# A GRU with its logits: two operands of the state update moved to PSUM, and gathers without their waits on single pieces of TensorE's work

## The reference

```python
x = emb_table[input_ids]                       # 2048 x 50 x 128
xp = einsum('bth,hk->btk', x, kernel) + b_i    # 384 columns: z, r, h
def step(h, xt):
    rec = h @ rec_kernel + b_r
    z = sigmoid(xz + rz);  r = sigmoid(xr + rr)
    hh = tanh(xh + r * rh)
    return z * h + (1.0 - z) * hh
last = state at the last position of the mask
logits = last @ emb_table.T                    # 2048 x 12501, float32
```

## Time and profile before

| | |
|---|---|
| Median of 3 runs | 1263.59 us (1258.02, 1263.59, 1264.37) |
| The profiled execution's own time | 1257.24 us |
| Its span in the profile | 1255.4 us |
| Mean granted clock of PE | 0.983 of full speed |
| Busy: PE, DVE, ACT, POOL | 86%, 64%, 56%, 65% |
| DMA queues: gathers (software), SP's (hardware) | 43.3%, 30.5% of 16 engines' span |

### The profile page before, as it was taken

One profiled execution on the slowest core, in us unless ns is written; L12 is line 12 of the kernel. 1 busy time (PEld: TensorE's weight loads), 2 busy tenths in 40 slices (PEclk: granted clock), 3 DMA queues, 4 the chain that ended last, 5 costly groups with the idle time before them and its releaser, 6 DMA issues.

```text
span 1255.4 us, 17436 instructions
## 1 busy us (share of the span) xinstructions
PE 1078.9 (86%) x6040; PEld 809.2 (64%) x6040; DVE 808.3 (64%) x1491; ACT 697.7 (56%) x1203; POOL 811.1 (65%) x812
## 2 busy tenths in 40 slices
PE   7956778777777777788889999999999999999997
PEld 6853444444444444444478888888887888988876
DVE  6634555555555555555578777778777777777654
ACT  3533334343434343344357777777777778888644
POOL 0007777777777777777777777777777776666100
PEclk9988999999999999999999999999999999999999
DMA  8975555555555555555578888888888889999799
GB/s 283 355 228 159 165 157 166 156 166 158 166 155 167 158 168 156 164 157 168 151 206 286 283 274 286 278 276 289 283 278 284 281 287 306 307 303 306 267 363 332
DMA packets 127494, 294.28 MB, mean 234 GB/s; under 512 B 18096, under 2 KB 33456, under 8 KB 127408
## 3 DMA queue, kind: packets, MB, share of 16 engines
q0 software_dynamic: 51200, 157.34, 43.3%
q1 hardware_dynamic: 76208, 135.84, 30.5%
HBM read 171.30 MB, written 121.81 MB: 233 GB/s over the span
## 4 chain that ended last, share of the span: by engine, by line
POOL 42%; PE 31%; issue 13%; DMA 10%; DVE 3%; ACT 1%; SPq 0%; DVEq 0%; POOLq 0%; ACTq 0%
POOL gathered L351 42%; DMA gathered<-gate_table,index 4%; PE x_ps L496 4%; PE x_ps L497 4%; PE x_ps L498 4%; DMA out_dram<-logits 3%; DMA gate_table<-gates 3%; PE r_ps L416 2%; PE r_ps L428 2%; PE z_ps L428 2%; PE c_ps L416 1%; PE z_ps L416 1%; PE c_ps L432 1%; PE c_ps L428 1%; PE c_ps L429 1%
## 5 line engine op out<-in xcount | busy, mean ns | idle before, releaser
L351 POOL DMA_INDIRECT gathered<-gate_table,index x800 | 809.2, 1011 | 357.5 <-issue 214.4
L601 ACT ACTIVATE gates<-r_ps,zr_bias 128x512 f32<-128x512 f32 (+1 forms) x250 | 151.1, 605 | 244.0 <-PE r_ps L423 191.5
L805 DVE SCALAR_TENSOR_TENSOR c_ps<-c_ps,bias_sb,gates 128x512 f32<-128x512 f32 (+1 forms) x250 | 162.3, 649 | 172.9 <-PE c_ps L423 128.3
L603 ACT ACTIVATE gates<-z_ps,zr_bias 128x512 f32<-128x512 f32 (+1 forms) x250 | 150.8, 603 | 188.3 <-PE z_ps L423 145.5
L416 PE MATMUL r_ps<-ident,gathered 128*128 128x128 f32 x800 | 111.5, 252 | 154.0 <-DMA gathered<-gate_table,index 153.5
L810 DVE TENSOR_TENSOR kept<-gates,state 128x512 f32<-128x512 f32 (+1 forms) x250 | 145.8, 583 | 118.1 <-ACT gates L603 118.1
L625 ACT ACTIVATE logits<-x_ps,nan_row 128x512 f32<-128x512 f32 (+1 forms) x300 | 197.3, 678 | 21.8 <-PE x_ps L498 20.9
L416 PEld LDWEIGHTS r_ps<-ident,gathered 128*128 128x128 f32 x800 | 84.5, 141 | 178.7 <-DMA gathered<-gate_table,index 153.2
L814 DVE SCALAR_TENSOR_TENSOR gates<-gates 128x512 f32<-128x512 f32 (+1 forms) x250 | 146.3, 585 | 57.8 <-ACT gates L607 56.7
L817 DVE TENSOR_TENSOR state<-kept,gates 128x512 f32<-128x512 f32 (+1 forms) x250 | 147.7, 591 | 26.4 <-DVE gates L814 0.5
L607 ACT ACTIVATE gates<-c_ps,bias_sb 128x512 f32<-128x512 f32 (+1 forms) x250 | 149.5, 598 | 16.2 <-PE c_ps L416 15.5
(11 more groups left out here) (100 smaller groups left out, 1570.9 us busy)
## 6 DMA issues: line engine op xcount, KB each, us to landing
out_dram<-logits SPq DMA_DIRECT2D x192, 512.0 KB, 4.3
gate_table<-gates SPq DMA_DIRECT2D x24, 768.0 KB, 4.2
gathered<-gate_table,index POOLq DMA_INDIRECT x800
emb_rows<-in_L_rec_emb_table_dram SPq DMA_DIRECT2D x48, 256.0 KB, 4.7
out_dram<-logits SPq DMA_DIRECT2D x8, 213.0 KB, 3.2
logits<-in_r_input_ids_dram SPq DMA_DIRECT2D x1, 400.0 KB, 6.0
logits<-in_r_input_mask_dram SPq DMA_DIRECT2D x1, 400.0 KB, 6.2
gate_table<-gates SPq DMA_DIRECT2D x2, 192.0 KB, 9.2
```

The costliest lines, as they stand in the source:

```text
L351: nc.gpsimd.indirect_dma_start(gathered[:, q, n, :].bitcast(F32), None, table, bass.IndirectOffsetOnAxis(ap=index[:, g, n:n + 1], axis=0)) ...
L601: nc.scalar.activation(r_sb[:, b, 0:width], r_ps[:, b, 0:width], ACT.Sigmoid, bias=zr_bias[:, 1:2]).then_inc(s_r, 1)
L603: nc.scalar.activation(z_sb[:, b, 0:width], z_ps[:, b, 0:width], ACT.Sigmoid, bias=zr_bias[:, 0:1]).then_inc(s_z, 1)
L805: nc.vector.scalar_tensor_tensor(out=c_bank, in0=c_bank, scalar=bias_sb[:, 1, 2:3], in1=r, op0=ALU.add, op1=ALU.mult).then_inc(s_scaled, 1)
```

## The change

Four edits, in three of the lists.
- z's sigmoid is written in place, into `z_ps`, and both uses of z on DVE (lines 810 and 814) read it there.
- new = (z - 1) * cand goes into the block's bank of `c_ps`, whose sum the tanh has read by then, and the last subtraction (line 817) takes it from there. The candidate itself stays in SBUF.
- The second, third and fourth gather of a block carry no wait. The constant `AHEAD` goes.
- The first gather's wait is written with other terms; (k - 1) * QS + q + 1 is the same number as g - QS + 1.

No instruction other than waits is added or removed, and no order changes.

```diff
-    AHEAD = QS - 1
...
-        z_sb, r_sb, cand = gates[:, 0], gates[:, 1], gates[:, 2]
+        r_sb, cand = gates[:, 1], gates[:, 2]
...
                 g = k * QS + q
-                ahead = g - AHEAD
                 if k > 0:
-                    pool.wait_ge(s_turned, g - QS + 1)
+                    pool.wait_ge(s_turned, (k - 1) * QS + q + 1)
                 for n in range(tiles_of(blk)):
-                    if ahead >= 0:
-                        if n == 1:
-                            pool.wait_ge(s_rec, 2 * ahead + 1)
-                        elif n == 2:
-                            pool.wait_ge(s_rec, 2 * ahead + 2)
-                        elif n == 3:
-                            pool.wait_ge(s_z_in, ahead + 1)
                     nc.gpsimd.indirect_dma_start(
...
                 act.wait_ge(s_z_in, g + 1)
-                nc.scalar.activation(z_sb[:, b, 0:width], z_ps[:, b, 0:width], ACT.Sigmoid, bias=zr_bias[:, 0:1]).then_inc(s_z, 1)
+                nc.scalar.activation(z_ps[:, b, 0:width], z_ps[:, b, 0:width], ACT.Sigmoid, bias=zr_bias[:, 0:1]).then_inc(s_z, 1)
...
-                z, r, new, kept_b, c_bank = (t[:, b, 0:width] for t in (z_sb, r_sb, cand, kept, c_ps))
+                z, r, new, kept_b, c_bank = (t[:, b, 0:width] for t in (z_ps, r_sb, cand, kept, c_ps))
...
-                nc.vector.scalar_tensor_tensor(out=new, in0=z, scalar=-1.0, in1=new, op0=ALU.add, op1=ALU.mult).then_inc(s_new, 1)
+                nc.vector.scalar_tensor_tensor(out=c_bank, in0=z, scalar=-1.0, in1=new, op0=ALU.add, op1=ALU.mult).then_inc(s_new, 1)
...
-                nc.vector.tensor_tensor(h, kept_b, new, ALU.subtract).then_inc(s_state, 1)
+                nc.vector.tensor_tensor(h, kept_b, c_bank, ALU.subtract).then_inc(s_state, 1)
```

## The result

| | before | after |
|---|---|---|
| Median | 1260.8 us (4 runs, 1255.42 to 1264.37) | 1216.91 us (4 runs, 1215.06 to 1218.09) |
| Ratio | | 0.9654, 95% interval 0.9612 to 0.9696 |
| Profiled execution: time, span | 1257.24, 1255.4 us | 1215.06, 1213.0 us |
| First stage, from PE's first block to its 101st | 529.1 us | 499.9 us |
| Second stage, to the 201st | 398.0 us | 383.6 us |

The forecast was 1217 us, with 1207 to 1237 around it. Of the 42.4 us by which the span fell, 29.2 come from the first stage and 14.4 from the second; the third and the start give 0.9, and the tail takes 2.1 back.

What follows compares the result with a forecast made beforehand. POOL's gathers were taken to bound the first two stages (to 1020 us), PE the third. 1257.24 - 28.4 (first stage) - 15 (second) = 1213.8 us, with 3.6 carried over 1217 us; range 1207 to 1237.

Steps and rivals of the forecast that it cites:

- POOL bounds both stages: First two stages, to 1020 us: POOL issues gathers without a pause, 528.8 of 529 us and 397.8 of 398.
- What stretches a gather: POOL beside DVE: two-SBUF-input instructions hold gathers at two points, early and 0.22 us before the end; single-SBUF-input ones don't.
- What line 817 says of an inference: Skill's inference that a tensor_tensor doesn't stall descriptor generation would mean no gain; 0.81 us after line 817 speaks against it.
- First stage, -28.4 us: First stage: all gather stretch goes, 400 x (1.017 - 0.946) = 28.4 us, POOL stays the bound; bounds 0 to 30.
- Second stage, -15 us, PE as the next bound: Second stage: of 22.5 us stretch, 15 gained, stage 383 us, the bound passing to PE; bounds 0 to 18.
- Third stage and after, 0: Third stage and after: PE has no idle time and unchanged work, so 0; shorter gathers only lengthen POOL's wait.
- Dearer operands, 0 with up to 65 ns for line 814: DVE's PSUM operands: 0 for lines 810 and 817, up to 65 ns for 814, hidden; 0, bounds -2 to +3.
- The waits, 0: Removed gather waits: cost nothing while POOL is behind PE, buffer gives nearly the same depth after; 0, bounds -1 to +3.
- Carrying 3.6 us over: Total: four earlier runs' mean lies 3.6 us above the profiled execution; added to 1213.8 us for 1217.
- The rival in which 817 alone keeps its hold: Line 817 still holds gathers, a third of both gains (14 us) goes, 1231 us; chance 0.04.
- The slower rival: Unpaced gathers delay output stores, deciding from about 11 us of landing; at 13 us, 74 us lost, 1291; chance 0.04.

Runs made afterwards that it cites:

- operands_more: Kernel before with z and new moved to PSUM, every gather wait kept, PE's marks on time: 1217.73 us against 1263.18, ratio 0.9637.
- second_paced: Changed kernel with the second, third and fourth gathers' waits put back for second and third stage alone, marks on time: 1218.07 us against 1263.18, ratio 0.9646.
- z_more: Kernel before with z alone in PSUM, new in SBUF, waits kept, marks on time: 1223.20 us against 1261.10, ratio 0.9687.
- operands_only: Kernel before with z and new moved to PSUM, every gather wait kept, PE's marks late: 1381.84 us against 1375.59, ratio 1.0038.
- after_again: The changed kernel itself once more, PE's marks late: 1426.76 us against 1381.12 for the kernel before, ratio 1.0325.

## Why the prediction was right

- **POOL bounds both stages.** Right. The first stage fell to 400 x 1.251 us when the gathers did, and PE still waited 119 us for them in it.
- **What stretches a gather.** Right for the instructions that were changed, and shown from both sides: taken away it goes, put back it returns, and it follows the inputs, not the output. Wrong in two things that didn't touch the sum. There is one point and not two: the 0.22 us behind line 814 were 0.82 behind line 810, and the gather at 409.62, given as one that line 805 left alone, had begun 0.15 us before that line, so at the one point nothing ran beside it; line 822 is the row that bears the reading. And a single SBUF input does hold a gather where the instruction is the state's copy (line 790), which caused 2.7 of the 2.9 us left in the second stage. The sum is safe since it took all stretch from the means (28.4 and 22.5 us) and not by points.
- **What line 817 says of an inference.** The Trainium skill (SBUF — State Buffer, "Who interferes with whom") infers that a `tensor_tensor` does not stall descriptor generation on POOL. The prediction took line 817's hold as speaking against it. The hold is real (the gather at 215.43 lost 0.37 us), but it comes 0.13 us into the gather, and later in it instructions with two SBUF inputs cost nothing; the gather also reads its indices from SBUF, and no run here shows which of its parts was held, so the inference is neither borne out nor refuted. That section's other rule in the Trainium skill, that a DVE instruction with two SBUF inputs contends with a GpSimd instruction that reads SBUF, agrees with every row here that has two.
- **First stage, -28.4 us.** 29.2 measured between PE's blocks.
- **Second stage, -15 us, PE as the next bound.** 14.4 measured; PE's pace of 7.60 us for a pair was the one forecast. My estimate of 0.02 us of remaining stretch for a gather was too high (2.9 us over 300, 0.010), but that changes nothing when PE is the bound.
- **Third stage and after, 0.** The third stage lost 0.5 us; what follows it took 2.1 more (82.2 against 80.1), which wasn't forecast and wasn't looked into.
- **Dearer operands, 0 with up to 65 ns for line 814.** 693 ns against 687 for new, 688 against 692 for h: 6 ns, not 65. The bound from line 805 was much too wide; that line also takes a scalar from SBUF, but whether this is what costs it 757 ns wasn't tried. ACT's z became 25 ns shorter (662 against 687).
- **The waits, 0.** Right by `operands_more` and `second_paced` while PE's marks are on time. Wrong where they are late, a case that the prediction didn't have.
- **Carrying 3.6 us over** from the profiled execution to the median: 1.9 measured (1216.91 - 1215.06). That the forecast of 1217 came out to 0.1 us is luck: the profiled execution was 1.3 us above the 1213.8 of the sum, and the carry 1.7 us below the 3.6.
- **The rival in which 817 alone keeps its hold**, priced at 1231: `z_more` is this case, and took 1223 in the median and 1233.6 in the profiled execution. In the first stage 11.8 of the 28.7 us stayed, not a third.
- **The slower rival** (stores landing late): the median landing went from 4.3 to 5.0 us, far below the 11 at which it would decide.

## What to carry to other kernels

When an engine issues without a pause and its instructions come in two lengths, look what runs beside the long ones, and measure from the other instruction's end to theirs: a constant distance (here 0.82 us) names a suspect. It isn't yet the cause: an instruction that always follows the culprit at once has a constant distance too (here 0.22 us). Count the cases in which the suspect ran at the same place and nothing happened. Price such a release stage by stage against the next bound, since edits don't add once that bound is reached. A wait that costs nothing while its engine is behind can still be worth keeping: with the waits the kernel measured the same in one condition and 3% better in the other.

## What the runs showed of the hardware

**PE's marks can come late.** In the first eight runs the five kernels that were also measured without this took 9% to 17% longer, all 43 executions of the kernel before beside them included (1369 to 1384 us), and in the last four they didn't; one chip was met under both conditions. The records say this much. In the profile of `operands_only`, PE's product for r was issued at 396.36 and its end is modelled at 397.45; ACT, free since 400.2, began r's sigmoid at 403.09, when the mark came (timeline, PE and ACT):

```profile
396.36 1.09 PE L423 MATMUL r_ps<-state,w_rec_sb 128*128 128x512 f32 x2
403.09 0.69 ACT L601 ACTIVATE gates<-r_ps,zr_bias 128x512 f32<-128x512 f32 x1 [2.87 <-remote]
```

The chain of the same profile, by engine: what released a waiting engine is often not found among the records, where the kernel before had none of it.

```profile
PE 48%; another core or an unknown queue 13%; issue 12%; ACT 12%; DVE 10%; DMA 5%; POOL 0%; DVEq 0%; SPq 0%; ACTq 0%; POOLq 0%
```

The trace records some 1030 marks of PE behind the table, and 414 of them come over 0.3 us behind the end of the matmul that sets them; in the profile of the kernel before it is none of 1420, and DVE's and ACT's marks are on time in both. By stage the late ones are 196 of 328, 190 of 412 and 28 of 178, and none of 108 in the logits behind. That fewer marks are recorded (DVE's and ACT's too) shows that these traces are less complete, and matmuls' ends are modelled, so whether the mark is late or the matmul can't be told from them. PE's granted clock was lower as well: 0.90 in the first stage and 0.985 in the second, where the same kernel with marks on time (`operands_more`) had 0.99 and 1.00. But the second stage took 459.2 us against 385.2, which a clock 1.5% lower doesn't explain. What delays the marks, and why the gathers' waits are worth 3% then (the kernel as changed at 1.0325, with waits at 1.0038), is not settled. In the second stage of `after_again` POOL waited 138.6 us for PE's c parts of four blocks back, in 53 waits of up to 4.2 us, and in `operands_only` 69.2 us in 46 of up to 1.8; that goes with gathers let out in bunches, but what is cause and what is effect wasn't tried.

**The gap between gathers is fixed.** 0.30 us, with a wait that is already over or with none, in all kernels. With 946 ns for a gather of 128 rows, POOL took 1.25 us for one wherever nothing held it, and the first stage now consists of 400 of these.

**What holds a gather.** Some 0.13 us after its start a gather stands still until a DVE instruction that already runs has ended, if that reads two tensors of SBUF or is the copy of the state from SBUF to SBUF; it then ends 0.82 us later. This held for 1126 of 1129 overlaps in the 14 traces.
